# GpSimd makes the first scan input of each state, and VectorE waits for the sums' DMAs themselves

## The reference, cut to what matters

```python
dA  = exp(dt_t[..., None] * A)                       # per channel and state
dBx = dt_t[..., None] * B_t[:, None, :] * x_t[..., None]
h   = dA * h + dBx                                   # recurrence over the 64 tokens
y   = einsum('bdn,bn->bd', h, C_t)                   # sum over the 16 states n
```

## Time and profile before

| | us |
|---|---|
| runs | 2396.54, 2399.12, 2408.80 (median 2399.12) |
| span of the profiled execution | 2396.3 |
| PE / DVE / ACT / POOL busy in it | 2107.1 / 1786.4 / 1059.8 / 588.9 |
| one pair of steps in the middle of a steady block | 44.69 |

### The profile page before, as it was taken

One profiled execution on the slowest core, in us unless ns is written; L12 is line 12 of the kernel. 1 busy time (PEld: TensorE's weight loads), 2 busy tenths in 40 slices (PEclk: granted clock), 3 DMA queues, 4 the chain that ended last, 5 costly groups with the idle time before them and its releaser, 6 DMA issues.

```text
span 2396.3 us, 27137 instructions
## 1 busy us (share of the span) xinstructions
PE 2107.1 (88%) x8244; PEld 1194.4 (50%) x8248; DVE 1786.4 (75%) x1801; ACT 1059.8 (44%) x2613; POOL 588.9 (25%) x405
## 2 busy tenths in 40 slices
PE   6877888989999979989999979989999987799987
PEld 2332453445555534445555534445555533577763
DVE  3499994389999975289999985279999984355533
ACT  2544441465565522365665522365655521243330
POOL 0099981001111120001111110001111120566530
PEclk9888999899999989899999989889999999799888
DMA  1468893148888771238888871238888772122210
GB/s 62 166 152 198 213 213 121 54 133 187 181 177 187 166 173 53 72 123 179 176 189 179 181 172 60 72 106 172 176 196 175 171 173 82 65 90 97 88 44 18
DMA packets 110074, 328.98 MB, mean 137 GB/s; under 512 B 12945, under 2 KB 13073, under 8 KB 107569
## 3 DMA queue, kind: packets, MB, share of 16 engines
q0 software_dynamic: 35328, 127.94, 28.7%
q1 hardware_dynamic: 68912, 189.58, 26.3%
q10 hardware_dynamic: 5760, 10.49, 1.2%
HBM read 183.00 MB, written 14.94 MB: 83 GB/s over the span
## 4 chain that ended last, share of the span: by engine, by line
DVE 40%; PE 31%; issue 18%; DMA 5%; ACT 3%; DVEq 1%; POOL 1%; SPq 1%; POOLq 0%; ACTq 0%; PEldq 0%
DVE hs L1130 13%; PE acc L1443 5%; DVE hs L1137 5%; DVE hs L1300 5%; PE pq L1488 4%; DMA xc<-hs 3%; DVE hs L1121 3%; DVE qr L1167 2%; PE pq L1732 2%; PE pq L1496 2%; PE pq L1526 2%; PE acc L1655 2%; PE pk L1732 2%; PE acc L1565 2%; DVE sc L1187 1%
## 5 line engine op out<-in xcount | busy, mean ns | idle before, releaser
L706 POOL DMA_DIRECT2D xc<-hs x192 | 165.8, 866 | 1301.6 <-DVE hs L1137 1263.9
L1130 DVE TENSOR_TENSOR_SCAN hs<-dA,hs 128x1024 f32<-128x1024 f32 x192 | 428.9, 2276 | 0.0
L888 ACT ACTIVATE dA<-dt,aneg 128x504 f32<-128x504 f32 x384 | 253.5, 707 | 250.9 <-DVE hs L1130 250.7
L1496 PE MATMUL pq<-qT,wa 128*128 128x512 f32 x768 | 354.8, 616 | 9.2 <-DVE sc L1187 9.2
L1576 PE MATMUL acc<-wb,oT 128*128 128x512 f32 x768 | 351.7, 602 | 3.6 <-ACT oT L876 3.6
L1137 DVE TENSOR_TENSOR hs<-hs,bc 128x1024 f32<-128x1024 f32 x256 | 307.9, 1205 | 2.2
L853 ACT ACTIVATE pr<-sc,mx 128x64 f32<-128x64 f32 x512 | 170.8, 335 | 247.4 <-DVE mx L1193 247.4
L1443 PE MATMUL acc<-xnT,wa 128*128 128x512 f32 x512 | 232.2, 607 | 11.5 <-PE acc L1443 4.4
L1496 PEld LDWEIGHTS pq<-qT,wa 128*128 128x128 f32 x768 | 146.9, 197 | 183.8 <-issue 173.7
L1121 DVE TENSOR_TENSOR hs<-u,bc 128x1024 f32<-128x1024 f32 x192 | 226.3, 1219 | 8.2 <-ACT xc L976 5.9
L1526 PE MATMUL pq<-kT,qp 128*128 128x64 f32 x1024 | 190.9, 289 | 41.2 <-DVE kT L1146 16.3
(11 more groups left out here) (200 smaller groups left out, 3312.7 us busy)
## 6 DMA issues: line engine op xcount, KB each, us to landing
xc<-hs POOLq DMA_DIRECT2D x240, 512.0 KB, 6.9
bc<-bc_rows SPq DMA_DIRECT2D x64, 512.0 KB, 7.5
wa<-in_wq SPq DMA_DIRECT2D x64, 512.0 KB, 10.2
wb<-in_wo SPq DMA_DIRECT2D x64, 512.0 KB, 5.8
wa<-in_wx SPq DMA_DIRECT2D x16, 512.0 KB, 4.2
wa<-in_wz SPq DMA_DIRECT2D x16, 512.0 KB, 4.9
wb<-in_ow SPq DMA_DIRECT2D x16, 512.0 KB, 7.2
k<-k_rows SPq DMA_DIRECT2D x32, 256.0 KB, 11.1
```

The source lines that it names most:

```text
L888: ins = S.activation(to[:, :, 1:SEQ], dt[:, s, :].rearrange("p (b t) -> p b t", t=SEQ)[:, :, 1:SEQ], ACT.Exp, scale=aneg[:, s, bass.ds(jj ...
L1130: V.tensor_tensor_scan(out=hs[:, c, :], data0=dA[:, c % 2, :], data1=hs[:, c, :], initial=0.0, op0=ALU.mult, op1=ALU.add).then_inc(scd.sem, 1)
L1496: ins = M.matmul(pq[:, h, :], wa4(p)[:, k, h * P:(h + 1) * P], qT[:, k, :], start=(k == 0), stop=(k == KE - 1))
```

## The change

Per state, VectorE's scan input of chunk 0 goes away. GpSimd makes it into a new buffer `uin` (128x1024, float32) by `feed_first`, after the DMA issue of chunk 3 of the state before; the scan of chunk 0 reads `uin` and still writes `hs[0]`. For the first state of a block `feed_first` runs as soon as the first chunk of `u` and the state's `bc` are there. The relays `landed` and their semaphore `yad` are gone: VectorE waits for `s_y[c]` itself, for chunks 1 to 3 at the scan input, for chunk 0 at the scan, and at the final gating. `steps` writes jj = 0 out and loops over 1 to 6.

```diff
+        uin = sb("uin", [P, CW])
...
-            with eng.Fori(0, NS // 2 - 1) as jj:
+            one(0, 0, False)
+            one(0, 1, False)
+            with eng.Fori(1, NS // 2 - 1) as jj:
...
-                def landed(jj, p, c):
-
-                    eng.wait_ge(s_y[c], (i - (c == 0)) * (16 * NS) + jj * 32 + (16 * p + 16))
-                    eng.sem_inc(yad.sem, 1)
...
+                def feed_first(jj, p, first=False):
+
+                    eng.wait_ge(s_bc[p], i * (8 * NS) + jj * 16 + 16)
+                    hold(eng)
+                    if first:
+                        eng.wait_ge(ur.sem, ur.upto(i, 0))
+                    else:
+                        eng.wait_ge(scd.sem, scd.upto(i, NCH * (p - 1)) + jj * (2 * NCH))
+                    hold(eng)
+                    G.tensor_tensor(
+                        uin[:, :].rearrange("p (d t) -> p d t", t=T), u[:, 0:2, :],
+                        bc[:, p, 0:1, :].to_broadcast([P, 2, T]), ALU.mult).then_inc(in0.sem, 1)
+
+                def sum_y(jj, p, last=False):
...
                                     accum_op=ALU.add).then_inc(s_y[c], 16)
-                        if c >= 2:
-                            landed(jj, p, c - 2)
-                        elif not first:
-                            landed(jj - 1 if p == 0 else jj, 1 - p, c + 2)
+                    if not last:
+                        feed_first(jj + p, 1 - p)
...
             def scan_input(i, jj, p, c):
-                eng.wait_ge(yad.sem, yad.upto(i, NCH * (p - 1) + c) + jj * (2 * NCH))
+                if not (isinstance(jj, int) and jj == 0 and p == 0):
+                    eng.wait_ge(s_y[c], summed(i, c, p) + jj * 32)
...
             def scan(i, jj, p, c):
-                eng.wait_ge(inr.sem, inr.upto(i, NCH * p + c) + at)
+                if c == 0:
+                    if not (isinstance(jj, int) and jj == 0 and p == 0):
+                        eng.wait_ge(s_y[0], summed(i, 0, p) + jj * 32)
+                    eng.wait_ge(in0.sem, in0.upto(i - 1, p) + jj * 2)
...
-                V.tensor_tensor_scan(out=hs[:, c, :], data0=dA[:, c % 2, :], data1=hs[:, c, :], initial=0.0,
+                V.tensor_tensor_scan(out=hs[:, c, :], data0=dA[:, c % 2, :],
+                                     data1=uin[:, :] if c == 0 else hs[:, c, :], initial=0.0,
...
-                        scan_input(i, jj, p, 0)
                         scan_input(i, jj, p, 1)
```

More of the change, by code:

```diff
@@ L297, in build @@
         inr = stage("scan_input_ready", NS * NCH)
+        in0 = stage("first_input_ready", NS)
+        inl = stage("later_inputs_ready", NS * (NCH - 1))
         scd = stage("scan_done", NS * NCH)
         hcd = stage("state_times_c", NS * NCH)
-        yad = stage("y_added", NS * NCH)
         pid = stage("pos_index_ready", 1)
@@ L406, in wb_places, with summed @@
             return at_o, at_o + (W_DT if mamba else 0)
+        def summed(i, c, states):
+            return (i - (c == 0)) * (16 * NS) + 16 * states
         block = ctx.enter_context(nc.Block())
@@ L643, in _ @@
         def _(eng):
-            lead(eng, ln1r, ln2r, ln3r, wqh, wqs, woh, wos)
+            lead(eng, ln1r, ln2r, ln3r, wqh, wqs, woh, wos, in0)
             G = nc.gpsimd
@@ L694, in split_step @@
                         split_wo(jj, p + 1)
-                def landed(jj, p, c):
-                    eng.wait_ge(s_y[c], (i - (c == 0)) * (16 * NS) + jj * 32 + (16 * p + 16))
-                    eng.sem_inc(yad.sem, 1)
-                def sum_y(jj, p, first=False, last=False):
+                def feed_first(jj, p, first=False):
[10 more added lines that the diff above has]
+                def sum_y(jj, p, last=False):
                     for c in range(NCH):
@@ L746, in one @@
                         begin_sum(k, 0)
-                    for c in range(1, NCH):
-                        eng.wait_ge(s_y[c], 16 * NS)
-                    eng.sem_inc(yad.sem, NS * NCH)
                 if mamba and attn:
-                    eng.wait_ge(yad.sem, yad.upto(i, -1))
-                    hold(eng)
+                    feed_first(0, 0, first=True)
                     eng.wait_ge(y0r.sem, y0r.upto(i, NCH - 1))
                     hold(eng)
-                    sum_y(0, 0, first=True)
+                    sum_y(0, 0)
                     sum_y(0, 1)
@@ L762, in one @@
                     sum_y(NS // 2 - 1, 1, last=True)
-                    for c in (2, 3):
-                        landed(NS // 2 - 1, 1, c)
                 if not mamba:
-                    eng.wait_ge(yad.sem, yad.upto(i - 1, NS * NCH - 1))
+                    for c in range(NCH):
+                        eng.wait_ge(s_y[c], summed(i - 1, c, NS))
                     split_wq(0, 0)
@@ L1038, in _ @@
         def _(eng):
-            lead(eng, ln1, ln1n, cv, ssv, ssi, sstr, spd, ur, inr, ch_n, ch_c, ch_f, scd, hcd, yad, pid, qt1, qt2, kt1, kt2, qrdy,
+            lead(eng, ln1, ln1n, cv, ssv, ssi, sstr, spd, ur, inr, inl, ch_n, ch_c, ch_f, scd, hcd, pid, qt1, qt2, kt1, kt2, qrdy,
                  krdy, q1r, q2r, srd, smx, rcp, prdy, x2r, ln3, ln3n, rmd, zgd, outr, ch_p, ch_a, yr, x1r,
@@ L1118, in scan_input @@
             def scan_input(i, jj, p, c):
-                eng.wait_ge(yad.sem, yad.upto(i, NCH * (p - 1) + c) + jj * (2 * NCH))
+                if not (isinstance(jj, int) and jj == 0 and p == 0):
+                    eng.wait_ge(s_y[c], summed(i, c, p) + jj * 32)
                 V.tensor_tensor(
                     hs[:, c, :].rearrange("p (d t) -> p d t", t=T), u[:, 2 * c:2 * c + 2, :],
-                    bc[:, p, 0:1, :].to_broadcast([P, 2, T]), ALU.mult).then_inc(inr.sem, 1)
+                    bc[:, p, 0:1, :].to_broadcast([P, 2, T]), ALU.mult).then_inc(inl.sem, 1)
             def scan(i, jj, p, c):
                 at = jj * (2 * NCH)
-                eng.wait_ge(inr.sem, inr.upto(i, NCH * p + c) + at)
+                if c == 0:
+                    if not (isinstance(jj, int) and jj == 0 and p == 0):
+                        eng.wait_ge(s_y[0], summed(i, 0, p) + jj * 32)
+                    eng.wait_ge(in0.sem, in0.upto(i - 1, p) + jj * 2)
+                else:
+                    eng.wait_ge(inl.sem, inl.upto(i - 1, (NCH - 1) * p + c - 1) + jj * (2 * (NCH - 1)))
                 eng.wait_ge(dar.sem, dar.upto(i, NCH * p + c) + at)
-                V.tensor_tensor_scan(out=hs[:, c, :], data0=dA[:, c % 2, :], data1=hs[:, c, :], initial=0.0,
+                V.tensor_tensor_scan(out=hs[:, c, :], data0=dA[:, c % 2, :],
+                                     data1=uin[:, :] if c == 0 else hs[:, c, :], initial=0.0,
                                      op0=ALU.mult, op1=ALU.add).then_inc(scd.sem, 1)
@@ L1320, in one @@
                         if attn and s % 2 == 0:
-                            eng.wait_ge(yad.sem, yad.upto(i, (NS - 1) * NCH + s // 2))
+                            eng.wait_ge(s_y[s // 2], summed(i, s // 2, NS))
                         elif s >= 2 and s % 2 == 0:
```

## The result

The changed kernel takes 2495.31 us (median of 4 runs, 2494.14 to 2497.25) where the kernel before took 2400.13: a ratio of 1.0393, with a 95% interval of 1.0372 to 1.0415. It is slower, as forecast, but by 95 us and not by 13. The profiled span grew from 2396.3 to 2491.8, and the mean granted clock of TensorE over the whole span fell from 0.942 to 0.908.

A forecast was written before the change was run, and what follows sets the result against it. VectorE was taken to bound the kernel, busy 44.59 of 44.69 us a pair. Pairs +9.2, heads +3.0, last state +1.3, relays -0.4 gave +13.1 us on the span, median 2412; range over all runs 2389 to 2426.

The forecast's parts named there:

- Odd scores to the next even ones: TensorE's stretch from odd step's scores to next even step's: 23.32 us, less 0.36 idle, 22.96.
- The loop itself: Five terms through four engines, scores to masked copy to GpSimd's product to keys to scores: 45.18 us, +0.49 a pair.
- VectorE's own chain: VectorE's work in a pair of steps, scan inputs saved against operations held up by GpSimd: +0.11 us a pair.
- 0.3 later: Bound for GpSimd's product starting only after the whole DMA issue of chunk 3: +0.7 us a pair on VectorE.
- The block: GpSimd's product holds up VectorE's keys' rotation in even steps: about 1.9 instead of 0.69 us, ending 0.54 after GpSimd.
- The head: Start of a steady block: the first product holds back VectorE's softplus chain, +1.0 us a block, +3.0 in all.
- The last state: Block's last state, without query work: scan waits for GpSimd's product, +1.5 us, counted in block 3 only as +1.3.
- The relays: VectorE's waits on GpSimd's relays removed: 0.4 us given back; the 16.5 before the gating stay, being DMA landing.
- What would show it: Signs: products about 2.35 us, keys 1.9, odd scan input 2.4, head operation 3.4, pair 45.2 with VectorE idle.
- Relieved: Rival: no block beside keys and scan input 1, so VectorE gains; -0.36 us a pair, median 2389; chance 0.16.
- Nothing happens: Rival: VectorE's chain at +0.11 us holds for all 24 pairs, TensorE's loop being shorter; median 2406; chance 0.27.
- The race is lost: Rival: GpSimd starts over 1.0 us late, scan input 1 goes first, +1.5 us a pair; median 2434; chance 0.07.

The follow-up runs named there:

- the kernel with two extra products: Changed kernel, with TensorE doing two extra matmuls with unused results while it waits for an odd step's keys: 2423.56 us, ratio 1.0102.
- even states alone: Changed kernel, but GpSimd makes chunk 0's scan input for even states only, VectorE that for odd states: 2408.93 us, ratio 1.0043.
- odd states only: Changed kernel, but GpSimd makes chunk 0's scan input for odd states only, VectorE that for even states: 2488.72 us, ratio 1.0367.
- late keys: Kernel before the change, without GpSimd product, with ScalarE making the keys' second half twice in sequence: 2483.03 us, ratio 1.0346.

## Why the prediction was wrong

*What failed.* The step is the loop's last long term, "Odd scores to the next even ones ... 23.32, of which the idle 0.36 can go: 22.96". I took it from the kernel before and let the keys move against it as if TensorE's durations stayed. They didn't: with the keys late TensorE idled 2.02 us, the clock went to the 1.2 GHz level, and the scores and the half projection in just that stretch ran slower, the scores' matmuls at 0.64 instead of 0.39 us. The term measured 25.98 us in the pair shown and 27.65 in the next (690.16 to 717.81), instead of 22.96. No step and no rival of the prediction speaks of the clock, which is to say that it was put at nothing; the "PEclk" of 1.00 stands in the earlier trace rows, and I read it as a constant. The price of the fall: the pair of 49.2 against 45.45 without it, 3.7 us, 21 times, some 78 us; the two medians give 72.

*The loop itself* was summed about right, but once the clock is held it is not what sets the pair. In the kernel with two extra products its five terms measure 4.15, 11.40, 3.68, 3.54 and 22.68 us, 45.45 in all against 45.18. But the first holds slack, 4.15 where 3.92 would do, since the masked copy doesn't wait there; and VectorE is busy for 45.35 us of that pair. So VectorE's own chain sets it, at +0.76 and not at the +0.11 of the forecast, and that 45.45 lies so near 45.18 is in part luck. The step that was off in both sums is GpSimd's start: I took 0.60 from the issue to the product and 2.35 for it, an end 2.95 after the issue's start. The trace has 635.07 and 638.30, 3.23. The product is recorded 0.56 after the issue's start and lasts 2.67, and this is what one sees if it can only run when the issue (0.85) is over: the "0.3 later" that I had kept as the bound, with +0.7 on VectorE's chain. The row in block 0 could not show it: VectorE's product with C, begun at 249.18 and 1.22 long, ended at 250.40 there, later than the issue (249.97), and would have held GpSimd in any case.

*The block* was as forecast: the keys operation 2.00 us ("about 1.9"), ending 0.57 after GpSimd (0.54). The odd step's net was forecast at +0.05, or 0.3 more with the later issue; even states alone show +0.37 in the pair, and the even step makes the rest of the +0.76, where +0.06 was forecast.

*The head.* In block 1 the softplus operation behind the first product took 3.37 us ("one operation at 3.4"), and the first state's scan starts at 518.65 instead of 517.67: +0.98, forecast +1.0. In blocks 2 and 3 the head can't be read alone: the stretch between two blocks' steps changed by +1.5 and -0.2.

*The last state.* In block 3 the scan waits 2.78 us and starts 4.00 after its scan input (2029.97 to 2033.97), where it was 2.27: +1.7, forecast +1.5. It starts 0.09 after GpSimd's end (2033.88), where I took 0.2.

*The relays.* Their removal brings nothing: the 16.5 us in front of the gating, with 4.1 of a DMA wait beside them, became 23.4 us of DMA waits, and the kernel with the direct waits alone measures the same as before. The 0.4 us given back are too small to be seen.

*What would show it.* Three signs came (products, keys, the head's operation), and the waits of VectorE before masked copy and query products too. The scan input of 2.4 in odd steps didn't, in this kernel: VectorE waited for the query projection, GpSimd's product was nearly over, and it took 1.41; with the clock held it took 2.73 (at 699.08). A pair near 45.2 (45.45) came only once TensorE was kept at work, and then without idle time of VectorE.

*The rivals.* "Relieved" is out: the keys are blocked. "Nothing happens" had VectorE's chain set the pair; with the clock held it does, but at +0.76 and not +0.11, and in the change itself TensorE's slowed loop sets it. "The race is lost" named a scan input going first, which happened only in a block's last state. It came closer in time, 2434, by another mechanism.

*What is left over.* In the change without the fall the profiled span is 23.8 us longer than before (2420.1). The steps of the three blocks, from the first even step's masked copy to the last, make 16.4 of it, the head of block 1 makes 1.1, and 5.6 lie between the steps of blocks 1 and 2 (236.47 us against 230.87); what makes these 5.6 has not been traced.

## What to carry to other kernels

Where VectorE sets the pace and TensorE follows at 95% busy, as here, a delay of what TensorE waits for can have two prices: the delay, and the granted clock of the work behind it. Look at how TensorE's idle time is spread and at the granted clock of each stretch, and when a forecast moves idle time together, take the durations behind it at both levels. Work given to GpSimd beside a busy VectorE belongs beside operations that read PSUM, held there by a wait; a place in the queue didn't keep it off the two-operand SBUF operations here.

## What the runs showed of the hardware

- The granted clock fell with TensorE busy for 287.58 of 310 us (block 1's steps in the change): after idle times of 1.04 and 2.02 us (the change), 1.10 and 2.02 (odd states only), 1.12 and 1.94 (late keys). It did not after 1.83 and 0.52 (even states only), nor after 1.44 and 0.52, nor even after 3.02 and 0.52 (even states only, the pair before, at 581.27 and 585.88); but with the product ahead of chunk 3's DMA it did after 1.05 and 0.82, and in the next pair, after 1.05 and 0.83, it did not. In the change it was low for 6.8 us in one pair (643.0 to 649.8) and for 10.2 in the next (690.8 to 701.0). The Trainium skill (TensorE: Matmul & The Clock Gate, "Part 1: The HAM clock gate") has two levels that follow how busy the engine has been; the two levels agree with the rows, and which pattern of idle time brings the lower one no run here settles.
- A GpSimd operation recorded as starting 0.3 us before the DMA issue ahead of it is over lasts longer by about that: 2.66 to 2.69 us behind an issue, 2.36 to 2.37 where it waited for the keys with the queue empty.
- Matmuls on ready data, over before TensorE's wait was, cost nothing here, and the clock stayed up: two of them (1.88 us together) in every pair were worth 72 us. Four (3.60 us) outlasted the wait, and were worth 61.
